# Second and third layer of a four-layer kernel as one section of heads and pieces

## The reference: four layers on the same 1024 rows

```
# layer 2: 16 heads of width 16, keys and values from the normalised context
kv = layer_norm(ctx) ; q,k,v = x @ Wq.T, kv @ Wk.T, kv @ Wv.T
x  = x + tanh(gate) * (softmax(q k^T / 4, masked) v) @ Wo.T
# layer 3: 32 query heads of width 8 on 8 key/value heads, keys and values from ctx itself
q,k,v = x @ Wq + bq, ctx @ Wk + bk, ctx @ Wv + bv
x  = (softmax(q k^T / sqrt(8) + mask) v) @ Wo + bo + x
out = (x - mean) * rsqrt(var + 1e-6) * gamma + beta      # over the 256 numbers of a row
```

## Time and profile before

| what | us |
|---|---|
| median of 3 runs | 1299.11 |
| profiled execution, its own time | 1306.43 |
| its span, first to last instruction | 1304.7 |
| layers 0 and 1 in it | 0 to 945 |
| context norm, loads, projections and stacks of layer 2 | 946.1 to 997.3 |
| attention of layer 2 (64 heads) | 997.3 to 1077.4 |
| output of layer 2, turn, projections and stacks of layer 3 | 1077.4 to 1129.4 |
| attention of layer 3 (128 heads) | 1129.4 to 1271.2 |
| output of layer 3, final norm, store | 1271.2 to 1304.7 |

### The profile page before, as it was taken

The page is one execution under the profiler, slowest core; times in us unless marked ns, Lnnn a source line. Parts: engine busy times, 40 slices in busy tenths (PEclk is TensorE's granted clock), DMA queues, the critical chain, the costliest instruction groups (busy, mean ns, idle before and its releaser), DMA issues. The chain is left out here.

```text
span 1304.7 us, 20610 instructions
## 1 busy us (share of the span) xinstructions
PE 1163.8 (89%) x7388; PEld 903.4 (69%) x7388; DVE 852.4 (65%) x2097; ACT 638.6 (49%) x1428; POOL 655.9 (50%) x677
## 2 busy tenths in 40 slices
PE   6999999999999999999999769986768998899994
PEld 4788888888888888888788624433436765666664
DVE  6776665766756766667756555985545657666756
ACT  3655655556655565455662114203133672477770
POOL 3665665556646565466763032770022661277760
PEclk9999999999999999999999869998888999899997
DMA  6210121112210112012102000000020000000000
GB/s 205 66 49 17 66 65 49 48 35 65 66 49 21 62 65 66 23 43 65 65 18 80 17 0 1 1 0 1 0 90 1 2 2 1 1 1 2 2 2 33
DMA packets 35110, 47.05 MB, mean 36 GB/s; under 512 B 3865, under 2 KB 22082, under 8 KB 35010
## 3 DMA queue, kind: packets, MB, share of 16 engines
q1 hardware_dynamic: 34640, 44.83, 10.7%
q10 hardware_dynamic: 370, 0.91, 0.2%
HBM read 44.69 MB, written 1.05 MB: 35 GB/s over the span
## 5 line engine op out<-in xcount | busy, mean ns | idle before, releaser
L444 POOL TENSOR_TENSOR a_prob<-a_prob,a_inv_total 128x512 f32<-128x512 f32 x128 | 144.3, 1127 | 208.3 <-DVE a_inv_total L732 208.3
L1583 POOL TENSOR_TENSOR l_scores<-l_scores,l_neg_max 128x512 f32<-128x512 f32 x144 | 147.8, 1041 | 103.1 <-DVE l_neg_max L1573 102.8
L1573 DVE CUSTOM_DVE_ANT_0 l_scores<-psum,mask 128x256 f32<-128x256 f32 x384 | 139.8, 421 | 72.9 <-PE psum L1526 72.9
L637 ACT ACTIVATE a_prob<-psum,a_neg_max 128x257 f32<-128x257 f32 x256 | 119.2, 473 | 94.2 <-DVE a_neg_max L729 93.5
L1604 ACT ACTIVATE l_prob_T<-psum 128x512 f32<-128x512 f32 x192 | 108.8, 590 | 37.2 <-PE psum L1540 37.2
L1540 PE MATMUL psum<-ident,l_scores 128*128 128x128 f32 x768 | 117.8, 292 | 7.3 <-POOL l_scores L1583 4.3
L1540 PEld LDWEIGHTS psum<-ident,l_scores 128*128 128x128 f32 x768 | 86.3, 147 | 42.1 <-issue 19.8
L736 DVE TENSOR_TENSOR a_probT_lo<-psum,a_probT_hi 128x512 fp32r<-128x512 f32 x128 | 88.0, 688 | 32.7 <-ACT a_probT_hi L641 32.1
L566 PE MATMUL psum<-ident,a_prob 128*128 128x128 f32 x512 | 77.8, 274 | 24.1 <-DVE a_probT_lo L736 21.7
L566 PEld LDWEIGHTS psum<-ident,a_prob 128*128 128x128 f32 x512 | 60.0, 140 | 44.7 <-issue 21.2
L729 DVE TENSOR_REDUCE a_neg_max<-psum 128x2 f32<-128x514 f32 x128 | 87.3, 682 | 1.2 <-PE psum L486 1.2
(11 more groups left out here) (331 smaller groups left out, 3294.9 us busy)
## 6 DMA issues: line engine op xcount, KB each, us to landing
wk_raw<-in_L_xattn_wk SPq DMA_DIRECT2D x16, 512.0 KB, 6.4
wq_raw<-in_L_xattn_wq SPq DMA_DIRECT2D x16, 512.0 KB, 5.7
wv_raw<-in_L_xattn_wv SPq DMA_DIRECT2D x16, 512.0 KB, 3.9
wo_raw<-in_L_xattn_wo SPq DMA_DIRECT2D x16, 512.0 KB, 4.0
ctx_rows<-in_ctx SPq DMA_DIRECT2D x3, 512.0 KB, 4.6
x_rows<-in_x SPq DMA_DIRECT2D x2, 512.0 KB, 9.6
mask<-in_mask_Bx1xSxS_ff SPq DMA_DIRECT2D x1, 1024.0 KB, 9.0
out_dram<-fin_y SPq DMA_DIRECT2D x4, 256.0 KB, 2.1
```

The source lines that it names most:

```text
L444: pool.tensor_tensor(prob[:, m % 4, :, 0:S], prob[:, m % 4, :, 0:S], rtot[:, m % 4, :].unsqueeze(2).to_broadcast([P, 2, S]), ALU.mult)
L637: act.activation(prob[:, m % 4, q, 0:S + 1], s_bank(g)[:, q, 0:S + 1], ACT.Exp, bias=negm[:, m % 4, q:q + 1], accum_out=tot[:, m % 4, q:q ...
L1573: e = dve.tensor_tensor_reduce(sc[:, i % SC, q, :], s_bank(i)[:, q * S:(q + 1) * S], masks[:, b * NM + q % NM, :], 1.0, BIG, ALU.add, ALU. ...
L1583: pool.tensor_tensor(sc[:, i % SC, :, :], sc[:, i % SC, :, :], m[:, i % SC, :].unsqueeze(2).to_broadcast([P, 2, S]), ALU.subtract).then_in ...
```

## The change

The stages of layers 2 and 3 become one `Block` (the new `layers_2_and_3`). `last_layers_orders` writes out one order of work for TensorE, ScalarE and VectorE: a loop over all 192 heads (64 of layer 2, then 128 of layer 3), and "pieces" of the other stages behind the turns of given heads. A piece is one PSUM bank of work and its eviction. Their names: XT2, XT3, CT, AT (x, context, normalised context turned), Q, K, V (projections), SQ, SK (stacks), OT (sums turned back, two or four per batch), OB (the result turned), OP (output projection). 24 pieces stand ahead of the loop and 4 between its first scores and its first turn. 60 stand behind heads of layer 2: heads 0 to 25, 28 to 57 and 60 to 63, one each. 40 stand behind heads of layer 3: heads 64 to 71 one each, then only behind odd ones (73 to 95, 99 to 109, 131 to 141, 163 to 173, 179 and 181). 4 end the program. The pieces in the loop all use PSUM bank 7, and a piece waits until the one before it is evicted. Sums have one bank instead of two.

Q, K and stacks are made for half the rows (two batches) at a time. In layer 3 all stack pieces are evicted by ScalarE (`evictor`), and `on_scalar` is false for every head, so GpSimd shifts all 128. The selection matrices, the ones, the scaling of Wq and bq, and the negated mask are GpSimd's. bo is added by GpSimd. The final norm is done batch by batch: VectorE the moments behind OP and the normalised rows later, GpSimd the power, scale and offset, and for the last batch scale and offset on VectorE. Each load has its own semaphore.

```diff
-        on_act = lambda i: i % 4 == 2
+def on_scalar(i):
+    return i < N2 and i % 4 == 2
...
+    opening = [('XT2', 0, c) for c in range(NC)] + [('CT', 0, c) for c in range(NC)] + [('Q', 2, 0, c) for c in range(NC)]
+    opening += [('XT2', 1, c) for c in range(NC)] + [('AT', 0, c) for c in range(NC)] + [('K', 2, 0, c) for c in range(NC)]
+    opening += [('SQ', 2, 0, g) for g in range(4)] + [('SK', 2, 0, g) for g in range(8)]
+    second = [('V', 2, 0, 0), ('V', 2, 0, 1), ('AT', 1, 0), ('AT', 1, 1)]
...
+    put(73, [('SK', 3, 1, 7)] + [('Q', 3, 1, c) for c in range(NC)] + [('SQ', 3, 1, g) for g in range(8)] + [('V', 3, 1, 0)], 2)
+    put(99, output_pieces(3, 0), 2)
+    put(131, output_pieces(3, 1), 2)
...
+    for i in range(HEADS):
+        pe.append(('T', i))
+        if i in behind:
+            pe.append(('F', behind[i]))
+        if i % 2 and i // 2 + 2 < HEADS // 2:
+            pe.append(('S', i // 2 + 2))
+        if i % 4 == 1 and i > 4:
+            pe.append(('A', i // 4 - 1))
...
+def evictor(p):
+    if p[0] in ('XT2', 'XT3', 'CT', 'AT', 'OB'):
+        return 'act'
+    if p[0] in ('SQ', 'SK'):
+        return 'act' if p[1] == 3 or p[3] % 2 == 0 else 'dve'
+    return 'dve'
...
+                def piece(p):
+                    kind, bank = p[0], ps[:, bank_of[p], :]
+                    if earlier[p]:
+                        landed(pe, [earlier[p]])
...
+                clear(spare[0][:, 0:768].bitcast(F32))
+                choose2()
+                pool.wait_ge(ld['q2'], 16)
+                pool.tensor_scalar(w2[:, 0], w2[:, 0], -SMALL[2].scale, None, ALU.mult).then_inc(scaled, 1)
+                ln.gpsimd(pool)
...
+                for i in range(HEADS):
+                    if not on_scalar(i):
+                        pool.wait_ge(s_read, i + 1)
+                        pool.tensor_tensor(sc[:, i % SC, :, :], sc[:, i % SC, :, :],
+                                           m[:, i % SC, :].unsqueeze(2).to_broadcast([P, 2, S]), ALU.subtract).then_inc(shifted, 1)
+                    extras(i)
```

More of the change, by code:

```diff
@@ L1577, in _ @@
-            @block.gpsimd
-            def _(pool):
-                for i in range(N):
-                    if on_act(i):
-                        continue
-                    pool.wait_ge(s_read, i + 1)
-                    pool.tensor_tensor(sc[:, i % SC, :, :], sc[:, i % SC, :, :],
-                                       m[:, i % SC, :].unsqueeze(2).to_broadcast([P, 2, S]), ALU.subtract).then_inc(shifted, 1)
+                for kind, what in pe_order:
+                    if kind == 'F':
+                        if what == output_pieces(3, 3)[2]:
+                            pe.wait_ge(s_read, HEADS)
+                        piece(what)
+                    elif kind == 'S':
+                        scores(what)
+                    elif kind == 'T':
+                        turn(what)
+                    else:
+                        sums(what)
@@ L1597, in shift, with exp @@
                     e.then_inc(act_shifted, 1)
-                shift(2)
-                for i in range(N):
+                def exp(i):
                     act.wait_ge(turned, i + 1)
@@ new lines, in final @@
+                def final(b):
+                    dve.wait_ge(rstd_ok, b + 1)
+                    for j in (2 * b, 2 * b + 1):
+                        dve.tensor_scalar(y[:, b % 2, j % 2, :], chip.x[:, j, :], mv[:, j, 0:1], rstd[:, j:j + 1], ALU.subtract, ALU.mult).then_inc(y_ok, 1)
+                    if b == B - 1:
+                        scale_and_offset(dve, b)
+                for kind, what in dve_order:
+                    if kind == 'E':
+                        evict(what)
+                    elif kind == 'max':
+                        maximum(what)
+                    elif kind == 'statistics':
+                        ln.statistics(dve, what)
+                    elif kind == 'normalise':
+                        ln.normalise(dve, what)
+                    elif kind == 'mask':
+                        make_mask()
+                    elif kind == 'moments':
+                        moments(what)
+                    else:
+                        final(what)
```

855 lines of the change are left out of this document (477 added, 378 removed).

## The result

The changed kernel takes 1316.97 us (median of 4 runs, 1315.52 to 1322.78). The kernel before, run beside it on the same chip, takes 1299.47 (4 runs, 1298 to 1301). The ratio of the means, with a fifth execution of 1319.57 in it, is 1.0145, 95% interval 1.0116 to 1.0174: 1.45% slower, where the prediction said 1275 and 1249 to 1295.

What follows compares the result with a forecast made beforehand. No engine is full in layer 3, latency binds; idle TensorE time outside the attentions was to be won. Opening 24, layer 2 121, layer 3 175, end 14 sum to 334 for 358.6, hence 1275 us, range 1249 to 1295.

Steps and rivals of the forecast that it cites:

- 10 projections of four 512- or eight 256-column halves at 0.88 (16 in 7.03): Layer 2 loop: TensorE's price for ten projection pieces, 0.88 us each, within 31.4 us for all 60 pieces.
- three OP at 0.87, one V of 0.95: Layer 2 loop: TensorE's price in us for three output projection pieces and one V piece, within the 31.4.
- The 32 stack pieces: Layer 2 loop: 12 K and 12 Q stack pieces at 0.46 us and eight at 0.23, within the 31.4.
- The opening: From 946.1 us to layer 2's first turn: a dependent chain of 24 us, bounds 20 and 28, now 54.0.
- 30 such pairs: 12: Layer 2: the second piece of each pair is 0.4 us late, behind ScalarE's exponential and eviction; 12 us of waits.
- one slow beginning of 4.1: Layer 2: its first eight heads run at clock 0.50, adding 4.1 us to 70.9.
- Rival 4: TensorE stays at half clock to head 24 of layer 2, +8 for pieces besides: 1291 us; chance 0.1.
- The period without pieces: Layer 3: 4.35 us per four heads against 4.18, with all four shifts on GpSimd; 5 us lost in all.
- a batch of the output: Layer 3: output pieces and final norm add 8.4 us for each of batches 0 to 2, 25.2 in all.
- rival 2: Layer 3: a GpSimd shift costs 1.29 us, not 1.04, a period 5.4, and the kernel is slower: 1308; chance 0.06.
- rival 3: Port lock: VectorE's two normalised-row instructions a batch wait up to 1.04 us each for GpSimd's shifts: 1282; chance 0.2.
- The end: After the last exponentials: a dependent chain for one batch, 14 us in place of 2.5 + 33.5.

Runs made afterwards that it cites:

- e10: e5 with the matmuls of the eight Q and K pieces inside layer 2's loop issued twice; 1311.01 us, ratio 1.0077.
- e1: The changed kernel with ScalarE's layer 2 shift of head 4k+2 behind, not ahead of, the exponential and eviction of head 4k; 1305.97 us, ratio 1.0039.
- e2: The changed kernel with GpSimd shifting all heads of layer 2 too, ScalarE none; 1305.73 us, ratio 1.0043.
- e5: The changed kernel with the edits of e1 and e3 together: every fourth shift on ScalarE in both layers, behind the exponential of head 4k; 1296.05 us, ratio 0.9971.
- e6: The changed kernel with three extra identity products on TensorE behind each odd head of layer 2, before its piece; 1323.47 us, ratio 1.0186.
- e3: The changed kernel with ScalarE shifting every fourth head in layer 3 too, as in the kernel before; 1310.68 us, ratio 1.0079.
- e8: e1 with the final norm's moments and normalised rows spread over several heads' maxima, scale and offset 16 heads behind the output projection; 1303.30 us, ratio 1.003.
- e7: e1 with the piece of every even head moved ahead of that head's turn; 1299.30 us, ratio 1.0002.

## Why the prediction was wrong, point by point

**The first failed step: "10 projections of four 512- or eight 256-column halves at 0.88 (16 in 7.03)", and "three OP at 0.87, one V of 0.95".** The price was half of what a piece takes. Two records belong to a float32 matmul, so the earlier trace rows are four pieces in 7.03, 1.76 each, and e10 measures 1.7 to 1.8. The quoted words contradict themselves: four of sixteen records in 7.03 are 1.76. The 14 pieces in layer 2 were each 0.87 to 0.95 too cheap: 12.4 us. In layer 3 there are seven (Q, V, OP): 6.2 us. It could have been seen from the rows, by holding the count of records against the count that the program's loops give.

A second price in the same sum was too small. The 32 stack pieces took TensorE 18.7 us in e1's layer 2, from start to next start without the idle time, where the prediction has 12.9: one that splits into high and low takes 0.62 here (1042.59 to 1043.21), not 0.46. The 0.46 is from a row in which such matmuls stand one behind the other, and in the loop each piece stands between others. All 60 pieces took 51.5 us there, for the prediction's 31.4.

The opening's late share is largely the same price, partly at 1.2 GHz. Its rows, TensorE's and one of VectorE (the normalising of the context):

```profile
947.54 5.40 PE L1571 MATMUL psum<-x_T,l_w 128*128 128x512 f32 x8 [2.36 <-POOL l_w L1955]
948.53 2.05 DVE L133 TENSOR_SCALAR prob_T<-ctx_rows,ln_ctx_mean_var,ln_ctx_rstd 128x256 f32<-128x256 f32 x4 [1.59 <-POOL ln_ctx_rstd L112]
953.65 1.04 PE L1584 MATMUL psum<-ident,prob_T 128*128 128x128 f32 x8
955.99 3.67 PE L1571 MATMUL psum<-ctx_normed_T,l_w 128*128 128x512 f32 x8 [1.30 <-ACT ctx_normed_T L1718]
966.81 1.25 PE L1661 MATMUL psum<-k_stack,q_stack 32*128 32x256 f32 x16 [1.99 <-DVE k_stack L1792]
967.99 6.04 PE L1607 MATMUL psum<-l_w,ctx_normed_T 128*128 128x256 f32 x16
975.34 0.66 PE L1677 MATMUL psum<-ident,scores 128*128 128x128 f32 x4 [0.43 <-ACT ctx_normed_T L1718]
```

Counted from the start of the stretch (943.2), K's projection began at 12.8 where I had 8.9, the scores at 23.6 where I had 18.3, the first turn at 32.1 where I had 24. So 3.9 were lost ahead of K, 1.4 at K and its split, and 2.8 at the scores, V and AT pieces: the granted clock was 0.50 over the scores and 0.61 from 968 to 974, and the two V pieces took 6.04. The first 3.9 are TensorE's, which the sum had free there. GpSimd's power ended 6.4 after the start (6.3 predicted) and the normalised rows were there at 950.6, but TensorE was in the two Q pieces until 952.8, 5.2 us, in part at the lower clock, and turned x before it turned those rows (953.65).

**The second failed step: "30 such pairs: 12", with "ScalarE first does the exponential" and "then the eviction".** There was a third instruction ahead of both, the shift of head 4k+2. I read the order of TensorE, which the shift's edit does not touch, and not what stands in ScalarE's queue between a turn and its piece's eviction. Idle time in layer 2 is 22.9 against the 14.5 that I had (12 + 2.5). With the shift behind the exponential it is 13.2 (e1): the estimate was near for the queue that I had in mind. (The stated bound of 24 for the waits did hold.) The busy time beside it can be added up too: 121 less 14.5 of waits and 4.1 of a slow beginning, plus 12.4, is 114.8, against 120.2 in e1. The remaining 5.4 are about what the stack pieces took more than priced, 18.7 for 12.9.

**What the waits bring with them.** I had one slow beginning of 4.1, and as a rival a slow stretch to head 24. In fact the granted clock fell to 0.50 in five spells of 3.4 us each in layer 2, from 1000.0, 1017.1, 1054.6, 1085.4 and 1095.6 on, 0.94 on average. In e1, e2 and e5, which have the shorter waits, and in e6, which fills them with work, it was 1.00. That is 8.1 us of busy time. How many spells there are is partly chance: e3, whose layer 2 has the same order and the same idle time, had three, and took 149.4 for 151.2. One of the five:

```profile
1017.10:1020.50 3.40, 3.40 (x22) 2.03 (x17) 0.74 (x4) 0.61 (x2) 1.04 (x1) 0.50 0.00 0
```

Rival 4 named the right thing in the wrong place and gave it 0.1.

So layer 2 comes out as 121 + 12.4 (Q, K, V and OP pieces) + 8.4 (waits) + 8.1 (clock) - 4.1 (the slow beginning, which did not occur as such) + 5.4 (stack pieces in the main) = 151.2.

**Layer 3: near in the sum, not in its parts.** Cut at the exponentials of heads 96, 128 and 160, it looks so (columns as above):

```profile
1127.20:1177.50 50.30, 47.22 (x394) 31.40 (x393) 27.15 (x137) 28.66 (x56) 33.72 (x33) 1.00 0.01 1
1177.50:1219.70 42.20, 38.24 (x348) 25.59 (x346) 28.30 (x145) 20.83 (x42) 35.36 (x35) 0.96 0.02 8
1219.70:1264.60 44.90, 41.02 (x348) 27.78 (x348) 28.16 (x145) 20.79 (x42) 35.49 (x36) 0.89 0.02 7
1264.60:1305.90 41.30, 37.59 (x344) 25.75 (x344) 26.97 (x138) 20.11 (x41) 33.62 (x34) 0.96 0.02 8
```

By the prediction's terms they were to take 43.6, 43.2, 43.2 and 45.0. The first, at full clock, is 6.7 longer, and 3.6 of that is the price of the four Q, V and OP pieces in it; the rest was not divided. In the other three TensorE ran at 1.2 GHz for 3.4, 10.2 and 3.4 us, for which the prediction has no term. What that costs is seen beside e3, whose layer 3 had no such spell: 164.1 us of busy time for 155.1, at the same idle time. Less half of the slow time, as an estimate, the three stretches are 40.5, 39.8 and 39.6, so the batches were priced some 3 us too dear each, or more. That the whole came out 3.7 from the forecast is luck: the clock's 9 and the 6.7 of the first stretch stand against the dear batches.

The period without pieces was 4.35 in the prediction. The changed kernel's PE, three scores one period apart, and GpSimd over that time:

```profile
1211.94 0.50 PE L1661 MATMUL psum<-k_stack,q_stack 32*128 32x256 f32 x4
...
1216.09 0.50 PE L1661 MATMUL psum<-k_stack,q_stack 32*128 32x256 f32 x4
...
1220.53 0.50 PE L1661 MATMUL psum<-k_stack,q_stack 32*128 32x256 f32 x4
```

```profile
1209.20 6.18 POOL L1962 TENSOR_TENSOR scores<-scores,neg_max 128x512 f32<-128x512 f32 x6
1215.80 7.18 POOL L1962 TENSOR_TENSOR scores<-scores,neg_max 128x512 f32<-128x512 f32 x7 [0.42 <-DVE neg_max L1833]
```

The two periods are 4.15 and 4.44, 4.30 on average, with GpSimd's shifts back to back at 1.03 each. The number agrees, but the reason is not borne out: e3, which gives GpSimd only three shifts of four, has the same 8.6 us for eight heads. So in such stretches the fourth shift is free, and the chain that I summed to 8.7 is not shown to be the limit. What makes 4.30 of the 4.19 before is open. What the fourth shift costs is paid at the batches: by e5 against e1 it is 9.9 us, where the prediction had 5.

For a batch of the output I had 8.4 us on top of eight periods, which is too much by the stretches above. Its single terms fit. The changed kernel's GpSimd around the first batch:

```profile
1196.64 2.04 POOL L1962 TENSOR_TENSOR scores<-scores,neg_max 128x512 f32<-128x512 f32 x2 [2.56 <-DVE neg_max L1833]
1198.64 0.72 POOL L1912 TENSOR_TENSOR fin_rstd<-fin_var_eps,minus_half 128x2 f32<-128x2 f32 x1
1199.34 1.04 POOL L1962 TENSOR_TENSOR scores<-scores,neg_max 128x512 f32<-128x512 f32 x1
1201.61 3.04 POOL L1962 TENSOR_TENSOR scores<-scores,neg_max 128x512 f32<-128x512 f32 x3 [1.24 <-DVE neg_max L1833]
1204.61 1.27 POOL L1536 TENSOR_TENSOR ctx_normed_T<-ctx_normed_T,rows_bc 128x512 f32<-128x512 f32 x1
1205.95 1.29 POOL L1538 TENSOR_TENSOR x_rows<-ctx_normed_T,rows_bc 128x512 f32<-128x512 f32 x1
```

The power is 0.72 (0.7 predicted), scale and offset 1.27 and 1.29 (1.3), and GpSimd idles 2.56 behind the output projection and its moments (2.3), then 1.24 behind the rows. The prediction adds them all up, and which of them overlap was not tried beyond e8.

**The rivals.** The dearer shift (rival 2) is refuted, by its group in the changed kernel's page (busy us, mean ns | idle before and what ended it):

```profile
L1962 POOL TENSOR_TENSOR scores<-scores,neg_max 128x512 f32<-128x512 f32 x176 | 179.2, 1040 | 142.7 <-DVE neg_max L1833 142.1
```

The kernel became slower by none of what this rival, the only one on that side, gave for a reason. The port lock (rival 3) is there and small. VectorE's two normalised rows at the batch above, where a shift of GpSimd had begun 0.06 before them, and all of them by line:

```profile
1199.40 1.45 DVE L1859 TENSOR_SCALAR ctx_normed_T<-x_rows,fin_mean_var,fin_rstd 128x256 f32<-128x256 f32 x2 [1.46 <-POOL fin_rstd L1912]
```

```profile
L1859 DVE TENSOR_SCALAR ctx_normed_T<-x_rows,fin_mean_var,fin_rstd x8: 400/412/1128, 1199.4 to 1316.6; 128x256 f32<-128x256 f32 x8
```

The pair took 1.45, where two of 0.41 would be about 0.8: one of the two waited, 0.7, not both for a whole shift, and so it was in each of the three batches. By this, rival 3 is some 2 us, not 7. The Trainium skill (SBUF — State Buffer, section Who interferes with whom) has the one that comes second blocked for the whole of the first one's instruction. This trace agrees that it stands: the long rows, 1.13 each with a median of 0.412, began 0.06 behind a shift's start and ended 0.15 behind its end (1199.40 + 1.13 against 1199.34 + 1.04).

**The end** took 15.1 for 14: the dependent chain was priced rightly, and it is the one place where the change does what it is for, 15.1 in place of 36.

**The range.** The sentence that above 1295 "only a dearer period in layer 3 can bring" it was wrong. The range had bounds for every unknown cost, but none for a known one that was misread, and for the waits only the eviction's own length (0.8 a pair). The 0.91 for the faster side came from a sum in which one term, 31.4 us of pieces, was 20 too small (12.4 of it by the halved price), and from rivals that all took that term as given.

## What to carry to other kernels

Before a row's time is divided by its count, hold the count against what the program's loops issue: in these traces a float32 matmul stands twice and a float32 transpose once, and a price that is off by two was on the path for every piece. Where stages are woven into a loop, read the queue of each engine between the release and the work that is waited for, not TensorE's order alone; an instruction that waits for something new must stand behind those whose inputs are there. An engine that the loop fills to the brim can keep the period and still cost time where irregular work has to pass: the period without pieces was the same with four and with three of four shifts on GpSimd, and yet the kernel with three was 10 us shorter (e5 against e1). And before a gain is put down to fewer waits, split it into idle and busy time: in e3 and in layer 3 of e7 all that the profiles show of it was the clock.

## What the runs showed of the hardware

- The granted clock fell to 0.50 for 3.4 us at a time, five times in layer 2 of the changed kernel, where TensorE was 85% busy and 11 of its waits were 1 us or more. With two such waits (e1) or with products put in their place (e6) it was 1.00 in the same stretch. Each of the five spells came soon after a wait of 0.9 to 1.5 us (one of 1.29 from 1052.0 on, say, ahead of the spell from 1054.6). But such a wait alone is not enough: e3, with the same 11, had three spells, and a wait of 1.61 in e7's layer 2 brought none.
- Such a spell in the changed kernel's layer 3, on PE, with a granted clock of 0.54 from 1205.0 to 1208.5:

```profile
1205.79 0.79 PE L1661 MATMUL psum<-k_stack,q_stack 32*128 32x256 f32 x4
1206.51 1.90 PE L1692 MATMUL psum<-prob_T,l_w 128*32 128x256 f32 x16
```

  The same scores took 0.43 and the same sums 1.00 in the earlier trace rows, from start to start; here 0.72 and 1.88. It follows the batch whose GpSimd rows stand above, with its waits of 2.56 and 1.24.

- What stays open: which part of e1's 17.8 us the clock would cost without the waits. The 9.7 of idle and 8.1 of busy time say how much of each there was, but only e6 took the spells away without the time of the waits, and there the filler took the place of both. What a stretch must look like for the clock to fall was not tried, and so the gains of e3 and e7 in layer 3 have no shown cause beyond the clock. Also open is why the period without pieces is 4.30 and not 4.19.
